# VectorE's ln_b addition of the second row half behind the quantisation of x, and ScalarE's square of it behind the square of the scan's input, in a post-LN decoder layer

## The reference, cut to what matters

```python
def _L0_ffn_ref(x, w1, b1, ln_g, ln_b, w2, b2):
    def bitlinear158(x, w, b):
        xq = act_quant(rms_norm(x))          # 8 bits, one scale a row
        wq = weight_quant(w)                 # -1, 0, 1
        return jnp.einsum('bsd,od->bso', xq, wq) + b
    h = jax.nn.silu(bitlinear158(x, w1, b1))
    h = jax.nn.gelu(h, approximate=False)
    h = layer_norm(h, ln_g, ln_b)            # 2048 columns
    return bitlinear158(h, w2, b2)
...
x = _layernorm(x + _L0_attn_ref(x, ...))
x = _layernorm(x + _L0_xattn_ref(x, ctx, ctx, decay))
x = _layernorm(x + _L0_ffn_ref(x, ...))
```

## Time and profile before

| what | value |
|---|---|
| median of 3 runs | 1053.55 us (1053.01 to 1054.15) |
| the profiled execution's own time | 1050.57 us |
| its span, first to last instruction | 1048.7 us |
| busy: PE, DVE, ACT, POOL | 945.9, 907.5, 827.6, 605.9 us |
| largest shares of the chain that ended last | DVE 34%, PE 28%, ACT 15%, issue 9%, POOL 7%, DMA 7% |

### The profile page before, as it was taken

How to read it: one execution, slowest core, us unless ns; L and a number is a source line. 1 busy time by engine, 2 the same in 40 slices (tenths; PEclk the granted TensorE clock), 3 DMA queues, 4 the chain that set the end, 5 groups by cost and what they waited for, 6 DMA issues and landing times.

```text
span 1048.7 us, 23313 instructions
## 1 busy us (share of the span) xinstructions
PE 945.9 (90%) x9260; PEld 650.5 (62%) x9260; DVE 907.5 (87%) x1490; ACT 827.6 (79%) x957; POOL 605.9 (58%) x767
## 2 busy tenths in 40 slices
PE   5998997999999999999999999999999999977515
PEld 3866756676677767676767766676767676644202
DVE  4678878999998999999999989999999999995766
ACT  3646686888979797988879897979888888977684
POOL 2332337474756759485756658494857576572643
PEclk9998998999999999999999999999999999988668
DMA  9432200223122121323131221323131321112213
GB/s 360 154 119 104 73 2 21 74 52 84 22 75 61 48 68 52 84 52 84 48 88 21 60 69 39 83 52 84 52 84 23 93 41 54 44 49 64 52 33 89
DMA packets 106352, 73.67 MB, mean 70 GB/s; under 512 B 91386, under 2 KB 91386, under 8 KB 104451
## 3 DMA queue, kind: packets, MB, share of 16 engines
q1 hardware_dynamic: 105522, 70.34, 24.4%
q10 hardware_dynamic: 720, 1.84, 0.5%
HBM read 41.73 MB, written 8.40 MB: 48 GB/s over the span
## 4 chain that ended last, share of the span: by engine, by line
DVE 34%; PE 28%; ACT 15%; issue 9%; POOL 7%; DMA 7%; SPq 1%; DVEq 0%; ACTq 0%; POOLq 0%
PE bank L1484 11%; PE bank L1345 7%; DVE neg_max L964 6%; DVE h L1095 6%; POOL h L549 5%; DMA xqT<-xq 5%; DVE stats L1021 3%; ACT h L725 3%; ACT junk L735 3%; ACT h L740 3%; PE bank L1485 3%; DVE fz L1100 2%; DVE qk_parts L987 2%; DVE rows L1037 2%; ACT L725 2%
## 5 line engine op out<-in xcount | busy, mean ns | idle before, releaser
L964 DVE TENSOR_REDUCE neg_max<-wave 128x8 f32<-128x2048 f32 x64 | 146.1, 2283 | 19.2 <-PE wave L1370 19.1
L549 POOL TENSOR_TENSOR h<-h,g_tile 128x2048 f32<-128x2048 f32 x30 | 139.4, 4645 | 39.1 <-ACT h L740 39.1
L657 ACT ACTIVATE probs<-wave 128x1024 f32<-128x1024 f32 x128 | 124.4, 1024 | 35.9 <-PE wave L1394 35.7
L1484 PE MATMUL bank<-w,xqT 128*128 128x512 fp8e4 x496 | 130.1, 386 | 23.7 <-DMA xqT<-xq 23.7
L439 POOL TENSOR_SCALAR attn_hi<-attn 128x256 fp32r<-128x256 f32 x64 | 30.2, 473 | 148.6 <-DVE attn L1003 132.9
L695 ACT ACTIVATE rows<-rows,rstd 128x512 f32<-128x512 f32 x96 | 74.3, 807 | 41.7 <-POOL rstd L455 23.8
L719 ACT ACTIVATE h<-bank,qx 128x512 f32<-128x512 f32 x124 | 83.9, 689 | 25.4 <-PE bank L1485 23.2
L1095 DVE TENSOR_TENSOR h<-h,b_tile 128x2048 f32<-128x2048 f32 x32 | 83.9, 2623 | 18.2 <-POOL h L549 18.1
L1484 PEld LDWEIGHTS bank<-w,xqT 128*128 128x128 bf16 x496 | 47.8, 99 | 81.4 <-issue 20.8
L1491 PE MATMUL bank<-w,hqT 128*128 128x512 fp8e4 x416 | 94.3, 380 | 0.2 <-DMA hqT<-h 0.2
L498 POOL TENSOR_TENSOR rows<-rows,bo_tile 128x512 f32<-128x512 f32 x32 | 51.6, 1633 | 71.1 <-DMA rows<-x 71.1
(11 more groups left out here) (184 smaller groups left out, 2841.9 us busy)
## 6 DMA issues: line engine op xcount, KB each, us to landing
ctx_sb<-ctxT SPq DMA_DIRECT2D x16, 512.0 KB, 3.7
rows<-x SPq DMA_DIRECT2D x16, 512.0 KB, 4.0
out<-rows SPq DMA_DIRECT2D x32, 256.0 KB, 2.5
xT_in<-xT SPq DMA_DIRECT2D x15, 512.0 KB, 4.7
h<-w1T SPq DMA_DIRECT2D x4, 1024.0 KB, 14.8
h<-w2T SPq DMA_DIRECT2D x4, 1024.0 KB, 4.9
h<-Wq SPq DMA_DIRECT2D x1, 1024.0 KB, 6.1
h<-Wk SPq DMA_DIRECT2D x1, 1024.0 KB, 9.7
```

The lines of the kernel that those rows point to most:

```text
L549: po.tensor_tensor(h_of(b, q)[:, :], h_of(b, q)[:, :], g_tile[:, :], ALU.mult).then_inc(done, 1)
L657: ac.activation(probs[:, kt, :, :], wave[:, :, kt * T:(kt + 1) * T], ACT.Exp, scale=SM_SCALE).then_inc(S["probs_ready"], 1)
L964: dv.tensor_reduce(neg_max[:, :, :], wave[:, :, :].rearrange("p j (t k) -> p j t k", t=NT), axis=AX_X, op=ALU.max, negate=True).then_inc(S ...
L1484: pe.matmul(p[:, :], xqT[:, q, kc, :], w1[:, kc, n * FW:(n + 1) * FW], start=(kc == 0), stop=False)
```

## The change

In VectorE's body the addition of ln_b to the second half of h of batch j - 2 goes from ahead of quantise_x(j - 1) to behind it. In ScalarE's body the square of that half goes from ahead of xq_store(j - 1) to behind ctx_square(j), directly ahead of zq_store(j - 2, 0). Nothing is added or removed, GpSimd, TensorE and SP keep their lists, and lead and drain stay as they are. It acts where batch j - 2 exists, in the 14 iterations j = 2 to 15.

```diff
@@ ScalarE, body @@
                 if alive(j, 0):
                     probs_of(j, 3)
-                if alive(j, 2):
-                    z_square(j - 2, 1)
                 if alive(j, 1):
                     xq_store(j - 1)
                 if alive(j, -1):
...
                 if alive(j, 0):
                     ctx_square(j)
                 if alive(j, 2):
+                    z_square(j - 2, 1)
                     zq_store(j - 2, 0)
@@ VectorE, body @@
                 if alive(j, 0):
                     attn_norm(j, 2)
-                if alive(j, 2):
-                    z_add(j - 2, 1)
                 if alive(j, 1):
                     quantise_x(j - 1)
                 if alive(j, 2):
+                    z_add(j - 2, 1)
                     quantise_z(j - 2, 0)
```

## The result

The changed kernel takes 1044.08 us (median of 4, 1043.21 to 1045.01) where the kernel before took 1053.85 (1053.01 to 1054.23): ratio 0.9905, 95% interval 0.989 to 0.9921. The profiled executions differ less: 1045.01 against 1050.57 us, 5.6 us.

The account below looks back on a forecast made before the run. TensorE and VectorE both near their bound, with the moved 2.28 us z_add on the chain; 2.3 (iterations 3 to 14) + 0.7 (long transpose) + 1.8 (iteration 15) = 4.8 us, so 1053.55 - 4.8 = 1048.7 us, range 1045.4 to 1052.2.

Parts of the forecast that it names:

- f 0 came only as early as TensorE allowed: At f group 0, TensorE is free at 599.50, so only 0.78 us of wait can go, not 2.20.
- silu 0 holds f 3: f group 3 needs the bank silu 0 reads, so an iteration gains 0.30 us, bounds 0.30 and 0.38.
- the square is hidden: ScalarE's square, 2.00 us with its read, fits in former idle time before zq_store, with 0.25 us to spare.
- One sign that the prediction named as speaking against it: The prediction is wrong if silu 0 comes earlier against z_add(0) than 602.39 did.
- the one long transpose: In one iteration xqT's transpose took 4.1 instead of 3.4 us; starting earlier covers that 0.7 us.
- 12 x 0.30 + 0.7: Iterations 3 to 14: 0.30 us gained each from f 3's earlier start, plus 0.7 us from covering the long transpose.
- the drain's 0.14: Hand-over from silu 0's end to f 3, taken as 0.14 us from a drain matmul; iteration 2 showed 0.06.
- the contention in quantise_x: GpSimd's earlier attn_split meets VectorE's small operations in quantise_x; taken as 0.11 us lost an iteration.
- the middle of two outcomes: At L1066, VectorE first leaves the roundings within 0.05 us; GpSimd first loses 0.24 us more; 0.11 taken.
- 1.8 us forecast: Iteration 15: f 3 starts at 949.37 + 0.69 + 0.14 + 0.24 = 950.44 instead of 952.23, carried to the end.
- it lies 2.98 us below the median of the runs: The kernel before's profiled 1050.57 us against its median; this difference was carried, turning 1045.8 into 1048.7 us.
- rival 1: TensorE's full wait is won, f 3 not held by silu 0: 0.78 us an iteration, 1041.3 us; chance 0.06.

Follow-up runs that it names:

- act_only: Kernel before with only ScalarE's move: the square directly ahead of zq_store, z_add left ahead of quantise_x; 1064.48 us against 1049.46, ratio 1.0137.
- silu0_first: Changed kernel with zq_store of the first half behind silu of group 0 instead of ahead of it; 1039.64 us against the changed kernel's 1043.08.
- silu0_rows: Changed kernel with silu 0 ahead of zq_store, and the next x's load ahead of the transposes of h in SP's queue; 1049.27 us, ratio 0.9968 to before.

## Why the prediction was right or wrong

**What bounds the kernel, and where the wait goes: right.** z_add was on the chain; f 0 came only as early as TensorE allowed; silu 0 holds f 3; the transpose is off the chain; the square is hidden with 0.22 us to spare (0.25 forecast). `act_only` and `silu0_first` show the hold of f 3 by itself, the two runs with the late transpose that this was on the chain and is nearly off it; the rest is read from the profile. One sign that the prediction named as speaking against it did come: silu 0 starts 31.55 us behind z_add(0), 0.2 earlier than the 31.75 before. It came from the contention, below, and not from another path.

**Iterations 3 to 14: mis-sized, 3.0 us with the one long transpose, measured 4.8.** From gelu of iteration 2 to that of iteration 14 it is 696.3 us in the profile of before and 692.3 in the first profile after, 696.9 and 692.1 as means over six and four profiles. The means, cut in two at silu 0, show both terms that were off:

- *Silu 0 to the next gelu*, 8.99 us before and 8.57 after: 5.1 us in twelve iterations, where the sum had 12 x 0.30 + 0.7 = 4.3. The hand-over from silu 0 to f 3 took 0.06 us (601.99 to 602.05), as iteration 2 had shown, and I had taken the drain's 0.14. The long transpose is covered, as forecast.
- *Gelu to silu 0*, 49.08 us before and 49.10 after: a loss of 0.3 us in all, where the sum had 12 x 0.11 = 1.3 for the contention in quantise_x. The prediction took the middle of two outcomes; the better one came in nine or ten of the twelve iterations, and its gain there (0.19 us in the iteration shown) was used up by the same kind of meeting elsewhere. VectorE now reaches the sum of the probabilities' halves sooner, against ScalarE's variance, and h_rstd's first step on GpSimd runs into it (0.42 us; 0.19 where nothing is in the way):

```profile
618.24 1.21 DVE L979 TENSOR_TENSOR x_round<-probs 128x1024 f32<-128x1024 f32 x1
```

```profile
619.08 0.42 POOL L534 TENSOR_SCALAR fs<-fs 128x1 f32<-128x1 f32 x1 [1.01 <-ACT junk L735]
```

**Iteration 15: right in size, in part by luck.** 1.8 us forecast; 58.47 to 56.77, and 58.33 to 56.75 as means: 1.6. The sum had 0.14 and a 0.24 that it doesn't explain behind silu 0, where the profile has 0.06; and silu 0 came 0.4 us later than forecast in the first profile, for there the contention was a loss (L1064 took 0.67 us instead of 0.47) and h_rstd's step ran into VectorE here too. The two errors nearly cancel. The drain behind it gained 0.4 us that I had at nothing.

**The step that failed is the last one: "it lies 2.98 us below the median of the runs, so I carry the difference".** Behind the lead the change is worth 6.8 us, 2.0 more than the 4.8 summed. The other 3 us of the 9.8 belong to the executions of the kernel before in that measurement, whose median lay 3.3 us over the profile, while the changed kernel's lay 0.9 below its own; the changed kernel's profile had a lead 1.2 us longer, and 3.3 + 0.9 - 1.2 makes the 3. Without the offset the forecast would have been 1045.8 us, against a measured 1044.08; with it, even the right sum of 6.8 would have given 1046.7. The offset was a property of one kernel's executions (the lead's scatter and the open part), and no constant to add to both. What it consists of stays open. The measured 1044.08 us lies nearer to rival 1 (1041.3) than to the forecast, but not by its mechanism: f 3 is held by silu 0 in 10 of the iterations 3 to 14 of the first profile, and an iteration gained 0.40 us in the mean, not 0.78.

The Trainium skill ("SBUF — State Buffer", Who interferes with whom) says that issue order decides who blocks. Every meeting read here agrees: L1067 and, in iteration 5, L1064 end with the operation of GpSimd that had started before them, and L534 with VectorE's L979, within 0.05 us; in `silu0_rows` L973 ends at 602.83, when the first of GpSimd's two additions in 2.49 us is over. Starts 0.04 us apart can't be forecast from the rows, so the sum had no better than the middle.

## What to carry to other kernels

When an operation on one engine reads what another engine writes, look at moving both: here one alone cost 15 us, the other alone 69, and both together gained 7 behind the lead. When a stall is cut, look for the next wait on the same queue: it was a PSUM bank three groups on, and freeing that gave 3.4 us more. Before moving work of GpSimd or VectorE by a microsecond, list the small operations of the other that lie at the new place; and don't carry one profile's distance from its median over to a changed kernel.

## What the runs showed of the hardware

- With the late transpose in the kernel before, TensorE's granted clock fell from its upper to its lower level at f 0 in 10 of 12 iterations, behind waits of 2.15 to 2.9 us, and not in the other two, behind 2.20 and 2.32. Behind the waits of 0.7 to 1.5 us in iterations 3 to 14 of the kernel before it didn't fall. Of the two stretches shown, the one with the fall was 1.5 us longer.
- In the ten profiles of the two kernels the first gelu, behind the lead, starts at 139.8 to 142.9 us. From the first gelu of iteration 2 to the end the times agree within 0.8 us in the six of the kernel before and within 0.4 us in the four of the changed one. Two profiles should be compared behind the lead.
- A few executions ran far longer: of five of VectorE's move alone, one took 1410 us at a granted clock of 0.65 and one 2362 us; of ten of `silu0_rows`, one took 1598 us at 0.56. What set them off isn't shown.
